# First head group's q and k built by matmuls at the start, the all-head projection moved behind the first score step, a second x buffer, and seven filler matmuls in the last batch

## The chip, the cores and the metric

The kernel runs on one core of one Trainium2 chip. The metric is device time in microseconds (us) of that core, as the median of repeated runs; lower is better. The kernels work on float32 data; matmul operands marked fp32r are float32 values read by TensorE in one pass, and precision is kept by splitting an operand into a high part (what fp32r keeps) and a low part (the rest), so that one product becomes three matmuls: high by high, high by low, low by high.

## What is computed

Eight batches of 512 tokens with 128 channels go through a macaron block: a feed-forward half step, an attention layer whose softmax is replaced by a normalised relu, and a second feed-forward half step.

```python
x = x + 0.5 * ffn(layernorm(x))                      # stage "pre" of the kernel
x = x + attention(layernorm(x))                      # 16 heads of 8 channels
x = x + 0.5 * ffn(layernorm(x))                      # stage "post"

def attention(x):
    qkv = (x @ w_qkv).reshape(B, S, 16, 24)          # q, k, v of 8 channels each
    w = relu(q @ k.T / sqrt(8))                      # 512 x 512 for each head
    out = (w / (w.sum(-1) + 1e-6)) @ v
    y = x + (out @ w_out + b_out)
    return (y - mean(y)) * rsqrt(var(y) + 1e-5) * gamma + beta

def ffn(x):                                          # 128 -> 512 -> 128, dequantised weights
    h = layernorm(x) * ln_gamma + ln_beta
    return x + 0.5 * (silu(h @ w1 + b1) @ w2 + b2)
```

## The kernel before, in words

**Attention.** The 16 heads form four groups of four. A group's q and k must lie in a form in which four heads occupy four blocks of 32 partitions (tiles `q_op` and `k_op`): each block holds the 8 channels of a head in four slots, which carry the high and low parts so that one 32-row matmul gives the sum of the products. TensorE (PE) first makes q and k of all heads at once (tasks `k` and `q`), ScalarE (ACT) copies the high part into `q_parts` and `k_parts`, VectorE (DVE) computes the low part beside it (`k_lo`, `q_lo`), and DMAs issued by SyncE (SP) spread them into `q_op` and `k_op`, four DMAs to a group.

**The loop.** A batch has 16 steps (four groups by four tiles of 128 keys). Step s issues four score matmuls (PE, line 454, into `scores`), then the value product of the step before (line 469, into `o_bank`). ACT applies the relu to two heads of a step (line 738) and DVE to the other two (line 1022). Beside these run the tasks of the neighbouring batches: the lists `PE_ORDER`, `ACT_ORDER`, `DVE_ORDER` and `POOL_ORDER` say for each step what an engine does for the batch after (`pre.*@1`) and the batch before (`post.*@-1`). Each engine runs its list strictly in the order written; semaphores order the engines. The last batch has no batch after it, so several of its steps hold only scores and values.

**The start.** Batch 0 has nothing before it to hide behind. Its `pre` stage runs by the lists `PE_FIRST`, `ACT_FIRST`, `DVE_FIRST` and `POOL_FIRST`, mostly in halves of 256 tokens (the last digit of a name). In order: `x_stats` and `x_apply` normalise, `hT` transposes, `fc1.f` multiplies (three matmuls, the third with the low part of hT), `fc2`, `xr` and `x1` form the residual, `u_apply` normalises again, `uT` transposes, then `k`, `q` and `v`. `weights.*` prepare the weights on DVE. `warm_up.n` are n matmuls of the identity with itself that have no other effect. `pre.hT@1` starts batch 1. The scores of step 0 wait until group 0's q, issued to DMA by ACT at line 703, has landed.

**The end.** `PE_LAST`, `ACT_LAST` and `DVE_LAST` finish the last batch's `post` stage in halves.

## Time and profile before

| | us |
|---|---|
| median of 3 runs | 381.1 |
| the runs | 381.10, 381.11, 379.63 |
| the profiled execution's own time | 381.01 |
| span of that execution, first to last instruction | 379.1 |
| mean granted TensorE clock | 0.991 of full |

| engine | busy us | share of the span |
|---|---|---|
| PE (matmul) | 368.6 | 97% |
| DVE | 289.8 | 76% |
| ACT | 226.6 | 60% |
| POOL | 218.5 | 58% |

Seven steady batches take 43.0 us each. The span is shorter than the device time by 1.9 us, which lie before the first and after the last recorded instruction. A busy PE in these tables counts a matmul that waits inside a group of four as busy, so 97% is not 97% of useful work. The chain that ended last runs over PE for 86% of the span; 2% are the DMA of q at the start.

### The profile page before, as it was taken

The numbers are of one execution on the slowest core, as the hardware profiler recorded it, in microseconds if no ns is written. First come the engines' busy times: TensorE is split into PE (matmuls) and PEld (weight loads), VectorE is DVE, ScalarE is ACT, GpSimd is POOL, SyncE is SP. The second block draws the span as 40 slices with busy tenths as digits, with TensorE's granted clock in tenths as the row PEclk, the third lists the DMA queues.
The fourth block names the chain that finished last, engine by engine and source line by source line (L and its number), as shares of the span: only waits on it lengthen the run. The fifth ranks groups of instructions, "written<-read, shape, count | busy, mean of one in ns | idle before, by whom it ended". The sixth has DMA issues, their size and how long they took to land.

```text
span 379.1 us, 11717 instructions
## 1 busy us (share of the span) xinstructions
PE 368.6 (97%) x4578; PEld 189.8 (50%) x4578; DVE 289.8 (76%) x698; ACT 226.6 (60%) x414; POOL 218.5 (58%) x448
## 2 busy tenths in 40 slices
PE   7979999999999999999999999999999999999997
PEld 7853524353564445553554445553454434523486
DVE  5744788897878978787878977788876976876684
ACT  3446456667846577566857476566857576465503
POOL 7674075638963589437972589438981566145041
PEclk9998999999999999999999999999999999999999
DMA  5165004500351006400361005400260005400001
GB/s 167 30 117 136 3 0 113 140 3 2 89 136 59 3 13 153 115 3 0 73 156 57 0 4 148 116 19 0 61 166 32 0 2 140 113 3 1 2 2 58
DMA packets 14390, 23.03 MB, mean 61 GB/s; under 512 B 2688, under 2 KB 3968, under 8 KB 14336
## 3 DMA queue, kind: packets, MB, share of 16 engines
q1 hardware_dynamic: 11440, 17.70, 19.1%
q10 hardware_dynamic: 2896, 4.59, 4.0%
q8 instruction: 36, 0.59, 0.7%
q14 instruction: 18, 0.15, 0.1%
HBM read 3.41 MB, written 2.10 MB: 15 GB/s over the span
## 4 chain that ended last, share of the span: by engine, by line
PE 86%; DVE 5%; DMA 3%; issue 2%; POOL 2%; ACT 1%; ACTq 0%; SPq 0%; DVEq 0%; POOLq 0%
PE o_bank L469 30%; PE scores L454 16%; PE pre_bank L412 10%; PE post_bank L412 9%; PE pre_bank L417 5%; PE pre_bank L418 3%; DMA q_op<-q_parts 2%; PE post_bank L417 2%; PE pre_bank L405 2%; PE pre_bank L431 2%; PE post_bank L431 2%; PE post_bank L418 2%; DVE probs L1022 1%; PE post_bank L405 1%; PE pre_bank L485 1%
## 5 line engine op out<-in xcount | busy, mean ns | idle before, releaser
L1022 DVE TENSOR_SCALAR probs<-scores 128x512 f32<-128x512 f32 x256 | 163.9, 682 | 50.1 <-PE scores L454 48.0
L738 ACT ACTIVATE probs<-scores 128x512 f32<-128x512 f32 x256 | 138.6, 595 | 68.9 <-PE scores L454 68.9
L469 PE MATMUL o_bank<-probs,v_op 128*32 128x512 f32 x1024 | 137.9, 611 | 0.0
L454 PE MATMUL scores<-q_op,k_op 32*128 32x512 f32 x512 | 78.4, 497 | 2.2 <-DMA q_op<-q_parts 1.7
L454 PEld LDWEIGHTS scores<-q_op,k_op 32*128 32x128 f32 x512 | 32.2, 182 | 87.2 <-issue 52.1
L628 ACT ACTIVATE pre_y<-pre_bank,b_sum,col_consts 128x512 f32<-128x512 f32 x28 | 21.8, 779 | 26.1 <-PE pre_bank L431 26.0
L469 PEld LDWEIGHTS o_bank<-probs,v_op 128*32 128x32 f32 x1024 | 21.7, 109 | 30.5 <-issue 24.5
L412 PE MATMUL pre_bank<-w,pre_y 128*32 128x128 f32 x960 | 30.8, 274 | 0.0
L412 PE MATMUL post_bank<-w,post_y 128*32 128x128 f32 x960 | 29.6, 273 | 0.0
L412 PEld LDWEIGHTS pre_bank<-w,pre_y 128*32 128x32 f32 x960 | 25.6, 110 | 7.8 <-issue 7.6
L412 PEld LDWEIGHTS post_bank<-w,post_y 128*32 128x32 f32 x960 | 26.2, 110 | 5.8 <-issue 5.7
L1051 POOL TENSOR_SCALAR norm_x_var<-norm_x_mv 128x4 f32<-128x4 f32 x21 | 4.1, 196 | 42.7 <-DVE norm_x_mv L804 42.0
L628 ACT ACTIVATE post_y<-post_bank,b_sum,col_consts 128x512 f32<-128x512 f32 x28 | 21.8, 778 | 3.5 <-PE post_bank L431 2.8
L1051 POOL TENSOR_SCALAR norm_y_var<-norm_y_mv 128x4 f32<-128x4 f32 x7 | 1.4, 199 | 37.7 <-DVE norm_y_mv L804 37.7
L1054 POOL TENSOR_TENSOR norm_x_rs<-norm_x_var,minus_half 128x4 f32<-128x4 f32 x21 | 21.2, 1010 | 1.7
L1178 POOL TENSOR_TENSOR y_rows<-y_rows,rows 128x512 f32<-128x512 f32 x7 | 9.0, 1292 | 21.0 <-ACT y_rows L662 21.0
L1132 POOL TENSOR_TENSOR v_op<-v_rows,v_op 128x128 f32<-128x128 f32 x32 | 13.7, 436 | 8.3 <-ACT v_rows L649 6.1
L1091 POOL TENSOR_TENSOR norm_x_rs<-norm_x_var,minus_half 128x4 f32<-128x4 f32 x16 | 16.4, 1024 | 1.3
L399 PE MATMUL o_bank<-ident 128*128 128x128 f32 x108 | 14.9, 300 | 1.6 <-POOL ident L1034 1.6
L399 PEld LDWEIGHTS o_bank<-ident 128*128 128x128 f32 x108 | 14.1, 213 | 2.2 <-POOL ident L1034 1.6
L1107 POOL TENSOR_SCALAR pre_xr<-pre_x,norm_x_mix 128x128 f32<-128x128 f32 x32 | 14.3, 459 | 0.8
L417 PE MATMUL pre_bank<-pre_t_hi,w_hi 128*128 128x512 f32 x28 | 14.2, 506 | 0.4 <-ACT pre_y L628 0.4
(188 smaller groups left out, 547.2 us busy)
## 6 DMA issues: line engine op xcount, KB each, us to landing
k_op<-k_parts SPq DMA_DIRECT2D x64, 128.0 KB, 2.7
q_op<-q_parts SPq DMA_DIRECT2D x62, 128.0 KB, 2.7
pre_x<-in_L_attn_x_dram ACTq DMA_DIRECT2D x7, 256.0 KB, 2.7
out_dram<-o_rows ACTq DMA_DIRECT2D x7, 256.0 KB, 2.0
w_int<-in_L_ffn_fc_q_dram SPq DMA_DIRECT2D x2, 256.0 KB, 3.9
rows<-in_lines_dram ACTq DMA_DIRECT2D x1, 256.0 KB, 5.2
s_rows<-in_L_ffn_fc_scales_dram SPq DMA_DIRECT2D x1, 256.0 KB, 6.2
q_op<-q_parts ACTq DMA_DIRECT2D x2, 128.0 KB, 3.6
```

The costliest lines, as they stand in the source:

```text
L399: mm(o_bank[1][:, 0:P], ident[:, :], ident[:, :], start=True, stop=True)
L412: last = mm(into[VW * j:VW * (j + 1), P * t:P * (t + 1)], tokens[:, part], w, start=start, stop=stop)
L417: mm(into, w_hi, t_hi, start=True, stop=False)
L418: mm(into, w_lo, t_hi, start=False, stop=False)
L431: mm(into, w1_hi[:, cols], st.t_lo[:, :], start=False, stop=True).then_inc(st.full, 1)
L454: mm(scores[i][:, j, :], k_op[rows, g, P * kt:P * (kt + 1)], q_op[rows, g, :], start=True, stop=True).then_inc(scores_done[i], 1)
L469: last = mm(o_bank[pair][VW * j:VW * (j + 1), :], v_op[:, kt, heads_of(g).start + 2 * j, :], probs[:, s % 2, j, :], start=(odd == 0 and kt ...
L628: activation(st.y[:, f, :], st.bank[:, :], ACT.Silu, bias=b1_sum[:, f:f + 1], scale=s1_col[:, f:f + 1]).then_inc(st.free, 1)
L738: activation(probs[:, s % 2, j, :], scores[0][:, j, :], ACT.Relu).then_inc(probs_done[0], 1)
L1022: v.tensor_scalar(probs[:, s % 2, 2 + j, :], scores[1][:, j, :], 0.0, None, ALU.max).then_inc(probs_done[1], 1)
L1054: p.tensor_tensor(norm.rs[:, i, :], norm.var[:, i, :], minus_half[:, i, :], ALU.pow).then_inc(norm.rs_in, 1)
L1091: p.tensor_tensor(norm.rs[:, 0, :], norm.var[:, 0, :], minus_half[:, 0, :], ALU.pow).then_inc(norm.half_in, 1)
```

## The change

Five things are changed together.

1. **Group 0 of batch 0 without copies.** POOL spreads the weights of group 0's q and k over the slots (`first_hi`, `first_lo`), so that matmuls give every slot the value directly; a per-partition factor (`sign_slot`, `low_slot`, made by DVE at the very start) turns two more passes, one by ACT and one by DVE, into the slot's high or low part, written straight into `q_op` and `k_op`. These are the parts `k0.0`, `q0.0`, `q0.1`, `k0.1`.
2. **All heads' q and k behind step 0.** `first.k.1`, `first.q.1` and `pre.hT@1` move from the start into new lists (`PE_BEGIN`, `ACT_BEGIN`, `DVE_BEGIN`) that run right after step 0 of batch 0, in full width of 512 tokens. SP copies groups 1 to 3 only. v is made in one piece of 512.
3. **A second x buffer.** Batch 1's x goes into its own buffer and is loaded by SP at the start; its statistics (`pre.x_stats@1`) move ahead of `first.xr.1` on DVE.
4. **fc1 in another order at both ends.** The high products of half 0 come first, the low products (`low.f.h`) after them, and `hT.1` stands behind half 0.
5. **Fillers.** In steps 3 to 8 and 10 of the last batch PE issues one identity matmul into the idle bank after the scores (`keep_warm`). The first warm-up stays at 12, the second goes from 9 to 7, those of 4 and 5 go, the last goes from 24 to 23.

```diff
+FIRST_PARTS = [("k0", 0), ("q0", 0), ("q0", 1), ("k0", 1)]
 PE_FIRST = [
-    "warm_up.12", "first.hT.0", "weights.b1", "first.hT.1", "first.fc1.0.0", "first.fc1.1.0", "first.fc1.0.1",
...
-    "first.fc2.3.1", "warm_up.9", "first.uT.0", "first.k.0", "first.q.0", "first.uT.1", "first.v.0", "first.k.1",
-    "first.q.1", "first.v.1", "warm_up.4", "pre.hT@1", "warm_up.5"
+    "first.fc2.3.1", "warm_up.7", "first.uT.0", "first.k0.0", "first.uT.1", "first.q0.0", "first.q0.1", "first.k0.1",
+    "first.v.1"
 ]
+PE_BEGIN = ["first.k.1", "first.q.1", "pre.hT@1"]
+BARE_STEPS = (3, 4, 5, 6, 7, 8, 10)
...
-    "pre.load_x", "weights.w1_hi", "first.hT.0", "first.hT.1", "first.fc1.0.1", "first.fc1.1.1",
-    "first.fc1.2.1", "first.fc1.3.1", "pre.load_x@1", "first.uT.0", "first.t_u.0", "first.k.0", "first.uT.1",
-    "first.q.0", "first.t_u.1", "first.k.1", "first.q.1", "first.v.0", "first.v.1", "pre.hT@1"
+    "weights.w1_hi", "first.hT.0", "first.hT.1", "first.fc1.0.1", "first.fc1.1.1",
+    "first.fc1.2.1", "first.fc1.3.1", "first.uT.0", "first.k0.0", "first.uT.1",
+    "first.t_u.0", "first.q0.0", "first.q0.1", "first.k0.1", "first.t_u.1", "first.v.1"
 ]
+ACT_BEGIN = ["first.k.1", "first.q.1", "pre.hT@1"]
...
+DVE_BEGIN = ["first.k_lo.1", "first.q_lo.1", "pre.hT@1"]
...
-    "first.x_stats.0", "first.x_stats.1", "pre.xr", "first.x1_stats.0", "first.x1_stats.1", "pre.x_stats@1",
+    "first.x_stats.0", "first.x_stats.1", "pre.xr", "weights.w_first", "first.x1_stats.0", "first.x1_stats.1", "pre.x_stats@1",
...
+            sp.dma_start(pre.x(1)[:, :, :], x_rows[1]).then_inc(x_loaded[1], 16)
...
+            def keep_warm(n):
+                pe.wait_ge(pre.free, len(PRE_FILLS) * B)
+                for _ in range(n):
+                    mm(pre.bank[:, 0:P], ident[:, :], ident[:, :], start=True, stop=True)
...
-                    pe.wait_ge(*emptied(pre, 1, "q"))
-                if kt == 0:
-                    pe.wait_ge(qk_in[g], 64 * (b + 1))
+                    pe.wait_ge(first_in, 3)
+                if b == 0 and s == TT // 2:
+                    pe.wait_ge(first_in, 4)
+                if kt == 0 and copied(g, b) > 0:
+                    pe.wait_ge(qk_in[g], copied(g, b))
...
+                    if b == 0 and s == 0:
+                        work(0, PE_BEGIN)
+                    if b == B - 1 and s in BARE_STEPS:
+                        keep_warm(1)
...
+                elif what in ("q0", "k0"):
+                    i = "qk".index(what[0])
+                    act.wait_ge(slots_ready, 2)
+                    act.wait_ge(first_made, FIRST_PARTS.index((what, h)) + 1)
+                    activation(first_high(i)[:, cols], first_bank(i, h), ACT.Copy, scale=sign_slot[:, i:i + 1]
+                               ).then_inc(first_high_in, 1)
...
+                    v.scalar_tensor_tensor((q_op, k_op)[i][:, 0, cols], first_bank(i, h), low_slot[:, i:i + 1],
+                                           first_high(i)[:, cols].bitcast(F32), ALU.mult, ALU.subtract).then_inc(first_in, 1)
...
+            def prepare_first():
+                pool.wait_ge(wqkv_ready, 1)
+                for to, of in ((first_hi, wqk_hi), (first_lo, wqk_lo)):
+                    last = p.tensor_copy(to[:, :, :].rearrange("p i (r c) -> p i r c", c=SLOTS),
+                                         of[:, :, 0:ROW].bitcast(F32).unsqueeze(3).to_broadcast([P, 2, ROW, SLOTS]))
+                last.then_inc(w_first_ready, 1)
```

How the change moves instructions shows in each engine's list. First DVE at the start, from the low part of the quantised fc1 weights (`w_lo`) to the residual; `pre_t_lo` is the low part of hT, `b_sum` the fc1 bias, `w<-w_int` the fc2 weights, `pre_xr` the residual. Before:

```order
L755 SCALAR_TENSOR_TENSOR w_lo<-w,col_consts,w_hi 128x512 [waits w_link]
L944 TENSOR_TENSOR pre_t_lo<-pre_bank,pre_t_hi 128x256 [waits pre_t_hi_first_half]
L762 TENSOR_TENSOR b_sum<-o_bank,col_consts 128x4 [waits cols_loaded,b1_added]
L764 TENSOR_TENSOR b_sum<-b_sum,col_consts 128x4 [waits b1_link]
L944 TENSOR_TENSOR pre_t_lo<-post_bank,pre_t_hi 128x256 [waits pre_t_hi_in]
L770 TENSOR_SCALAR w<-w_int 128x512 [waits w2_loaded]
...
L789 TENSOR_TENSOR wqk_lo<-wqk,wqk_hi 128x256 [waits wqk_link]
L926 SCALAR_TENSOR_TENSOR pre_xr<-rows,pre_xr 128x512 [waits rows_loaded,pre_mixed]
L949 TENSOR_TENSOR x<-pre_bank,pre_xr 128x256 [waits pre_residual,pre_full_first_half]
```

Now, on DVE in the same place:

```order
L841 SCALAR_TENSOR_TENSOR w_lo<-w,col_consts,w_hi 128x512 [waits w_link]
L1030 TENSOR_TENSOR pre_t_lo<-pre_bank,pre_t_hi 128x256 [waits pre_t_hi_first_half]
L997 TENSOR_SCALAR pre_h<-pre_x,norm_x_mv,norm_x_rs 128x128 [waits norm_x_rs_in,norm_x_measured]
...
L1030 TENSOR_TENSOR pre_t_lo<-post_bank,pre_t_hi 128x256 [waits pre_t_hi_in]
L848 TENSOR_TENSOR b_sum<-o_bank,col_consts 128x4 [waits cols_loaded,b1_added]
...
L856 TENSOR_SCALAR w<-w_int 128x512 [waits w2_loaded]
...
L875 TENSOR_TENSOR wqk_lo<-wqk,wqk_hi 128x256 [waits wqk_link]
L881 BN_STATS norm_x_stats<-pre_x 128x6 [waits x_loaded1]
...
L890 BN_AGGR norm_x_mv<-norm_x_stats 128x2 [waits norm_x_mix_in,norm_x_shift_in,norm_x_counted]
...
L1012 SCALAR_TENSOR_TENSOR pre_xr<-rows,pre_xr 128x512 [waits rows_loaded,pre_mixed]
L1035 TENSOR_TENSOR x<-pre_bank,pre_xr 128x256 [waits pre_residual,pre_full_first_half]
```

The weight preparations now stand behind the low part of hT's second half, and the statistics of batch 1's x stand ahead of the residual. Next PE, around step 0 of batch 0. Before:

```order
L412 MATMUL post_bank<-wv,t_u 32x128 [waits pre_bank_free]
...
L405 MATMUL pre_bank<-ident,pre_h 128x128 [waits pre_rows,pre_bank_free]
...
L454 MATMUL scores<-q_op,k_op 128x512 [waits qk_in0,pre_bank_free]
...
L417 MATMUL pre_bank<-pre_t_hi,w_hi 128x512 [waits pre_bank_free]
L418 MATMUL pre_bank<-pre_t_hi,w_lo 128x512
L431 MATMUL pre_bank<-pre_t_lo,w_hi 128x512
L454 MATMUL scores<-q_op,k_op 128x512 [waits probs_done0]
```

Now, on PE:

```order
L464 MATMUL pre_bank<-wv,t_u 32x128 [waits pre_bank_free,pre_free_first_half]
...
L508 MATMUL scores<-q_op,k_op 128x512 [waits first_in]
...
L469 MATMUL o_bank<-pre_t_hi,wqk_hi 128x512
L470 MATMUL o_bank<-pre_t_hi,wqk_lo 128x512
L629 MATMUL o_bank<-pre_t_lo,wqk_hi 128x512
L469 MATMUL post_bank<-pre_t_hi,wqk_hi 128x512
L470 MATMUL post_bank<-pre_t_hi,wqk_lo 128x512
L629 MATMUL post_bank<-pre_t_lo,wqk_hi 128x512
L457 MATMUL pre_bank<-ident,pre_h 128x128 [waits pre_rows,pre_bank_free]
...
L469 MATMUL pre_bank<-pre_t_hi,w_hi 128x512 [waits pre_bank_free]
```

The wait for the copies of group 0 (`qk_in0`) is gone from step 0, and six matmuls of 512 columns and the transposes of batch 1 now stand between step 0's scores and batch 1's first fc1, behind which step 1's scores come. The same place on ACT: before, the parts of q and k, the DMA and the v copies stand ahead of step 0's relus (`probs`).

```order
L695 ACTIVATE q_parts<-scores 128x256 [waits pre_bank_full]
L703 DMA q_op<-q_parts 64x1x512 [waits q_high_in,q_high_first_half]
L703 DMA q_op<-q_parts 64x1x512 [waits pre_bank_free,pre_free_first_half]
...
L624 ACTIVATE pre_t_hi<-pre_bank 128x512 [waits pre_bank_full]
L738 ACTIVATE probs<-scores 128x512 [waits scores_done0] x2
L628 ACTIVATE pre_y<-pre_bank,b_sum,col_consts 128x512 [waits pre_bank_full]
```

Now, on ACT:

```order
L779 ACTIVATE v_rows<-pre_bank 128x512 [waits pre_bank_full]
L808 ACTIVATE probs<-scores 128x512 [waits scores_done0] x2
L776 ACTIVATE k_parts<-o_bank 128x512 [waits pre_bank_full]
L776 ACTIVATE q_parts<-post_bank 128x512 [waits pre_bank_full]
L697 ACTIVATE pre_t_hi<-pre_bank 128x512 [waits pre_bank_full]
L701 ACTIVATE pre_y<-pre_bank,b_sum,col_consts 128x512 [waits pre_bank_full]
```

Three copies of 512 columns now stand between step 0's relus and batch 1's first silu.

## Rows read from the trace of the kernel before

**Rows 1.** The page: the granted TensorE clock in 40 slices.

```profile
PEclk9998999999999999999999999999999999999999
```

**Rows 2.** Chain that ended last, start: start us, length us, what.

```profile
14.74 2.20 PE o_bank L399 x18
...
20.80 0.36 ACT q_parts L695
...
21.99 4.35 DMA q_op<-q_parts
...
26.48 0.50 PE scores L454 x3
...
32.22 0.50 PE scores L454 x2
```

**Rows 3.** Stretches: length, busy PE PEld DVE ACT POOL, granted clock, DMA share, GB/s.

```profile
16.80:21.20 4.40, 3.84 (x50) 2.72 (x48) 3.18 (x15) 2.93 (x8) 3.66 (x11) 1.00 0.02 6
21.20:23.40 2.20, 1.20 (x13) 0.98 (x9) 0.41 (x2) 0.66 (x2) 0.41 (x1) 1.00 0.35 64
23.40:26.50 3.10, 1.79 (x18) 1.63 (x18) 0.69 (x1) 0.60 (x1) 2.66 (x8) 1.00 0.98 186
...
28.80:32.15 3.35, 3.35 (x12) 0.95 (x12) 0.86 (x2) 1.69 (x3) 3.35 (x4) 0.51 0.78 210
```

**Rows 4.** Timeline of DVE, start: start us, length us, [idle before <-releaser].

```profile
8.37 0.42 DVE L944 TENSOR_TENSOR pre_t_lo<-post_bank,pre_t_hi 128x256 fp32r<-128x256 f32 x1
...
12.46 0.69 DVE L926 SCALAR_TENSOR_TENSOR pre_xr<-rows,pre_xr 128x512 f32<-128x512 f32 x1 [1.22 <-POOL pre_xr L1107]
13.49 0.42 DVE L949 TENSOR_TENSOR x<-pre_bank,pre_xr 128x256 f32<-128x256 f32 x1 [0.34 <-PE pre_bank L412]
...
16.43 0.87 DVE L795 BATCH_NORM_STATS2 norm_x_stats<-pre_x 128x6 f32<-128x128 f32 x4
```

**Rows 5.** Timeline of ACT, start.

```profile
9.43 2.83 ACT L683 ACTIVATE pre_y<-scores,b_sum,col_consts 128x512 f32<-128x512 f32 x4 [1.42 <-PE scores L538]
...
26.98 1.09 ACT L738 ACTIVATE probs<-scores 128x512 f32<-128x512 f32 x2 [2.30 <-PE scores L454]
27.95 0.78 ACT L628 ACTIVATE pre_y<-pre_bank,b_sum,col_consts 128x512 f32<-128x512 f32 x1
```

**Rows 6.** Timeline of POOL, start.

```profile
7.11 0.79 POOL L1089 TENSOR_SCALAR norm_x_var<-norm_x_mv 128x4 f32<-128x4 f32 x1
...
24.00 0.20 POOL L1089 TENSOR_SCALAR norm_x_var<-norm_x_mv 128x4 f32<-128x4 f32 x1
```

**Rows 7.** Timeline of PE, start.

```profile
23.39 0.66 PE L405 MATMUL pre_bank<-ident,pre_h 128*128 128x128 f32 x4 [1.00 <-ACT v_rows L708]
...
33.54 1.07 PE L469 MATMUL o_bank<-probs,v_op 128*32 128x512 f32 x8
```

**Rows 8.** Timeline of PE, last batch, steps 8 to 10 (L454 scores, L469 values).

```profile
338.17 1.44 PE L454 MATMUL scores<-q_op,k_op 32*128 32x512 f32 x4
339.54 1.93 PE L469 MATMUL o_bank<-probs,v_op 128*32 128x512 f32 x8
341.40 0.80 PE L454 MATMUL scores<-q_op,k_op 32*128 32x512 f32 x4
342.13 1.43 PE L469 MATMUL o_bank<-probs,v_op 128*32 128x512 f32 x8
...
344.08 0.51 PE L454 MATMUL scores<-q_op,k_op 32*128 32x512 f32 x4
```

**Rows 9.** The same columns for a stretch of the last batch.

```profile
340.00:345.00 5.00, 5.00 (x36) 1.26 (x28) 1.98 (x4) 1.90 (x4) 4.64 (x12) 0.71 0.01 3
```

**Rows 10.** Timeline of DVE, last batch, steps 7 to 9.

```profile
337.80 2.61 DVE L1022 TENSOR_SCALAR probs<-scores 128x512 f32<-128x512 f32 x4
342.34 1.29 DVE L1022 TENSOR_SCALAR probs<-scores 128x512 f32<-128x512 f32 x2 [1.93 <-PE scores L454]
```

**Rows 11.** The page's DMA issues: KB each, us to landing.

```profile
w_raw<-in_L_attn_w_qkv_dram SPq DMA_DIRECT2D x1, 192.0 KB, 6.2
```

More of the change, by code:

```diff
@@ L30 @@
 ZERO_POINT = 128.0
+FIRST_FILLS = ["hT", "fc1.0", "fc1.1", "fc1.2", "fc1.3", "fc2", "uT", "v", "k", "q"]
 PRE_FILLS = ["hT", "fc1.0", "fc1.1", "fc1.2", "fc1.3", "fc2", "uT", "k", "q", "v"]
@@ L204, in build, with __init__ @@
         class Stage:
-            def __init__(self, n, fills):
+            def __init__(self, n, fills, buffers):
                 self.fills = fills
-                self.x = sb(f"{n}_x", [P, TT, D])
+                self.two_x = [sb(f"{n}_x{i}", [P, TT, D]) for i in range(buffers)]
                 self.h = sb(f"{n}_h", [P, TT, D])
@@ L536, in edge @@
                     two_products(to, w1_hi[:, weights], w1_lo[:, weights], st.t_hi[:, cols])
+                elif what.startswith("low"):
+                    f = int(what[-1])
+                    weights, to = slice(P * f, P * (f + 1)), scores[f // 2][:, f % 2, cols]
                     pe.wait_ge(*emptied(st, h, "hT"))
@@ L650, in task @@
                                    ).then_inc(pre.free, 1)
-                    elif what == "load_x" and b > 0:
-                        act.wait_ge(pre.rows, b)
-                        act.wait_ge(pre.res, b)
-                        act.dma_start(pre.x[:, :, :], x_rows[b]).then_inc(x_loaded, 16)
+                    elif what == "load_x" and b > 1:
+                        if b > 1:
+                            act.wait_ge(pre.rows, b - 1)
+                            act.wait_ge(pre.mixed, b - 1)
+                        act.dma_start(pre.x(b)[:, :, :], x_rows[b]).then_inc(x_loaded[b % 2], 16)
                     elif what in pre.fills:
@@ L738, in _ @@
                         activation(probs[:, s % 2, j, :], scores[0][:, j, :], ACT.Relu).then_inc(probs_done[0], 1)
+                    if b == 0 and s == 0:
+                        work(0, ACT_BEGIN)
                     work(b, beside)
@@ L1023, in _ @@
                                         ).then_inc(probs_done[1], 1)
+                    if b == 0 and s == 0:
+                        work(0, DVE_BEGIN)
                     work(b, beside)
@@ L1191, in work @@
                 for stage, what, tb in tasks(b, names):
-                    if (stage, what) == ("last", "mix"):
+                    if stage == "weights":
+                        prepare_first()
+                    elif (stage, what) == ("last", "mix"):
                         mix(norm_x2, tb)
```

173 lines of the change are left out of this document (107 added, 66 removed).

## The prediction

> **What bounds the kernel now.** I read the slices of the granted clock first, then the chain of waits, then timelines of the places the change touches. PE's clock is full but for one slice of 40 [rows 1], and the steady batches don't change: their PE order is the same, and PE is never waiting there for what the change moves. So only the start and the last batch can give time, and both give little: 26.5 us of the start lie before the first scores.
>
> At the start the chain runs from the high part of q (20.80) into the DMA of q, 4.35 us, and then the scores of step 0 at 26.48 [rows 2]. PE has little to do meanwhile: 1.20 of 2.20 us and 1.79 of 3.10 us busy, part of it warm-ups. Right after, from 28.80 to 32.15, its clock is 0.51, the lower of the two levels, 1.2 GHz [rows 3]. Step 2's scores come at 32.22 [rows 2]. That is the point to watch: from step 2 on the PE order is the same before and after, so the shift of step 2 is the shift of everything behind it.
>
> In the last batch a second stretch at the low level lies at about 339 to 342: the mean clock of 340 to 345 is 0.71 [rows 9], and the values of step 7 take 1.93 us [rows 8] where they take 1.07 at full clock [rows 7]. DVE then idles 1.93 us waiting for PE [rows 10]. So PE is the late one there.
>
> **The start, step by step.** Durations are those of the same operations before.
>
> *DVE, to the residual.* `hT.1` comes behind half 0 on PE. The fc1 products can begin near 7.1, since `w_lo` no longer waits behind `x_apply.1`; twelve of them at 0.12 us take 1.5, the transposes 0.4, ACT's copy 0.4, so DVE's low part of half 1 ends near 9.9, where it ended at 8.79 [rows 4]: 1.1 us later. The weight preparations stand behind it. Batch 1's statistics, about 1.2 us of DVE's time from 16.43 on [rows 4], are now ahead of the residual too. Against these 2.3 us stand the idle times of 1.22 and 0.34 us [rows 4], which are used up. What is left, with 0.2 for hand-overs, puts x1's first half at 14.4 rather than 13.49 [rows 4]: **0.95 us later**.
>
> *ACT's silus* start after the seventeenth product rather than the ninth, at 10.5 instead of 9.43, and end near 13.3 instead of 12.26 [rows 5]. fc2's last blocks move by 0.7, and DVE is the later one by then, so this adds nothing.
>
> *To step 0.* The statistics are gone from behind `u_apply.0`, but `u_apply.1` now stands ahead of uT's low part and waits for POOL. My chain: u_apply.0 16.8, uT.0 on PE 17.5, its low part 18.9, k0.0 19.4, uT.1's low part 20.6, q0.1 on PE 21.1, through ACT 21.5 and DVE 21.9, k0.1 22.25; `t_u.1` ends on ACT at 22.1. Scores would be free at 21.9, but the v product, 0.9 us, stands ahead of them on PE and waits for `t_u.1`: 22.2 to 23.1. **Step 0 at 23.1**, 3.4 us earlier than 26.48. The two copies of weights on POOL (1.5 us by the 0.79 us of its longest small operation and what 128x512 take, bounds 0.9 and 2.6) fit its idle time before x1's statistics.
>
> *To step 1.* Here most of it is given back. Before, batch 1's transposes (0.66 us, at 23.39 [rows 7]) lay under the DMA, and so did their parts. Now behind step 0's scores come k and q in full width (6 matmuls, 1.45 us) and these transposes on PE. ACT is later: v's copy ends at 23.95, two relus 1.09 [rows 5], then k, q and hT each 0.5 to 0.6, to 26.4. DVE follows with three low parts to 27.4. Batch 1's fc1.0 needs the last of them, and step 1's scores stand behind it at 27.74. Before, fc1.0 followed the scores at once and ACT's silu of it began at 27.95 [rows 5]; mine begins there too. So **the 3.4 us at step 0 are 0.1 at step 1**.
>
> *From step 1 to step 2.* Before, step 1's fc1 and values ran at the low clock. Their full durations (0.9 and 0.99 against 1.5 and 1.86, and the scores') make 1.54 us of the time to 32.22. With PE at full clock throughout, mine puts step 2 at 30.8: **1.4 us earlier**. But PE is nearly idle between the warm-ups (7 instead of 9, ending near 16.9) and v: about 1.9 us of work in 5.3, much less than the 2.99 of 5.3 that it did between 21.20 and 26.50, and the clock fell after those [rows 3]. So I expect a low stretch at the start again, only earlier. At worst it covers v, step 0 and the first of k: step 0 at 24.05, step 1 at 29.0, step 2 at 32.05, **0.1 us earlier**. At best it falls on small matmuls that wait anyway. I take 0.5 us earlier, nearer to the worst, since v and the scores are dense work right behind the idle time.
>
> *The copies* of groups 1 to 3 are issued after k's low part (26.1): four issues of 0.62 and a landing of up to 4.35 us [rows 2] make 33.1. Step 4 needs them at about 35.5. No wait.
>
> **A rule on shared ports.** While DVE computed `w_lo` from two operands in SBUF, POOL's small operation took 0.79 us at 7.11; alone it takes 0.20 at 24.00 [rows 6]. Such pairs delay each other. POOL's second weight copy may be running when DVE wants to begin the residual near 13.7, an operation with two SBUF inputs; no row shows which of the two would wait, so its price is 0 to 0.4 us at x1, inside my range. The Trainium skill (SBUF — State Buffer, "Who interferes with whom") says that whoever issues first holds the shared port pair for the whole instruction and the other fully blocks. By that rule the residual would wait for the copy, up to 0.4 us, and the sum would be 379.8 rather than 379.4.
>
> **The last batch.** A filler is one float32 matmul of 128 columns: 9 warm-ups took 2.20 us [rows 2], so 0.24 each, 1.7 for seven. Not all is paid. Where DVE has statistics or an addition besides its relus, PE waits inside a group of scores (1.44 us for 0.44 of work at 338.17 [rows 8]), and a filler before only shortens that wait. Going through steps 3 to 8, fillers add up to 0.5 us on PE by step 8, and DVE's two relu pairs from 337.80 to 340.41 [rows 10] absorb most. At full clock step 9's scores would come near 340.7 instead of 341.40, the values behind them at 341.2 to 342.2 instead of 342.13 to 343.50, and step 10 at 342.75 instead of 344.08 [rows 8]; with the filler of step 10, **1.1 us earlier**. If the fillers don't hold the clock, they cost 0.6.
>
> The reordered end (`PE_LAST`) is a wash: the first half's products start 0.4 us earlier, silu 0 can start 0.6 later, and fc2's final blocks meet both. I take 0, bounds -0.2 and +0.2. The earlier loads of later x change nothing: nobody waited for x in a steady batch.
>
> **The sum.** From the profiled execution, 381.01 (span 379.1 and 1.9 around it; the median is 381.1): 381.0 - 0.5 - 1.1 = **379.4 us**. About 0.5%, 1.9 us, is what a measurement of this kernel can tell from no change, so faster means below 379.2 and slower above 383.0.
>
> **The rivals.**
>
> *No low stretch on the path at either end.* The start gives 1.4 and the last batch 1.1: 378.5. For it: the new order does its dense work, v, step 0, k and q, in one row. Against: PE's idle start. Chance 0.22.
>
> *The fillers don't hold the clock.* Seven identity matmuls add 1.7 us of work over some 15. Then the end costs 0.6 instead of giving 1.1, and the start gives 0.5: 381.1. The warm-ups of the start are the same kind of matmul and stand for it, and the clock fell after 1.28 us of them all the same [rows 3]. Chance 0.20.
>
> *The wait only moves.* The copies of group 1 land after step 4 wants them, with a margin of 2.4 us that a landing of 6.8 us would use up. 1 us past that gives 380.4. Chance 0.05.
>
> *Slower: x of batch 1 lands late.* DVE takes batch 1's statistics ahead of the residual, so x's load, queued on SP behind the 192 KB of `w_raw`, holds up `xr.1`, x1 and everything behind them. It decides from a landing at 12.5; past 14.1 the kernel is slower than before. `w_raw` took 6.2 us to land [rows 11]. If x takes twice that from its issue near 3.1, it lands at 15.5 and the time is 382.4. Against it: 256 KB behind `w_raw` at the rate of the start is one or two us, so about 10. Together with further low stretches behind step 1 (1.5 us each), which act in the same direction, chance 0.08.
>
> **How the numbers follow.** The forecast's own case has 0.45, with 378.8 to 380.1 and two fifths of it below 379.2. Faster: 0.18 and 0.22, 0.40. Slower by over 0.5%: 0.05, a part of the last rival. Within: 0.55. For 8 in 10 the range must take in the case with no low stretch, down to 378.1 with its bounds of 0.4, and the fillers' failure up to 381.3.
>
> **What would show it.** In the changed profile: DVE's x1 at 14.4; PE's step 0 at 23 to 24 with no DMA ahead of it; step 1 near 27.7 to 29 with PE idle before fc1's low product, which waits for DVE's low part of batch 1's hT; a low stretch between 19 and 26 rather than 28.8 to 32.15; step 2 at 30.8 to 32.1. In the last batch, values of steps 7 and 8 at 1.07 us, and step 10 about 1.1 us nearer to the start of the batch's step 3. I would be wrong if the hand-overs at the start chain tighter than mine, so that step 1 follows step 0 by less than 4 us, or if the low stretch stays away.

## The result and the profile after

The changed kernel takes 386.5 us (median of 6 runs, 384.1 to 387.18), the kernel before 380.37 beside it (6 runs, 378.29 to 381.32): ratio 1.0161, 95% interval 1.0132 to 1.0190. It is 1.6% slower, outside the range of 378.1 to 381.3, on the side that had a chance of 0.05. The profiled execution took 386.52 with a span of 384.6. Two runs of the kernel before, of 384.17 and 436.22 us, were in a slower state of the chip and are left out of every figure below.

The page, as [rows 1]: the granted clock is low in two slices now.

```profile
PEclk9986999999999999999999999999999999999999
```

PE's start, as [rows 2, 7] (start us, length us, what, [idle before <-releaser]):

```profile
1.58 5.49 PE L445 MATMUL o_bank<-ident 128*128 128x128 f32 x24 [1.58 <-POOL ident L1129]
6.86 0.47 PE L581 MATMUL pre_bank<-ident,pre_h 128*128 128x128 f32 x2
...
23.72 1.62 PE L464 MATMUL pre_bank<-wv,t_u 128*32 128x128 f32 x32 [0.99 <-ACT t_u L766]
25.27 0.80 PE L508 MATMUL scores<-q_op,k_op 32*128 32x512 f32 x4
...
29.75 0.66 PE L457 MATMUL pre_bank<-ident,pre_h 128*128 128x128 f32 x4 [1.41 <-DVE q_parts L1056]
31.82 0.80 PE L469 MATMUL pre_bank<-pre_t_hi,w_hi 128*128 128x512 f32 x1 [1.41 <-DVE pre_t_lo L895]
...
33.40 0.80 PE L508 MATMUL scores<-q_op,k_op 32*128 32x512 f32 x4
...
35.91 1.94 PE L526 MATMUL o_bank<-probs,v_op 128*32 128x512 f32 x8
37.78 0.51 PE L508 MATMUL scores<-q_op,k_op 32*128 32x512 f32 x4
```

Step 0's scores stand at 25.27, 1.2 us earlier than in [rows 2], step 1's at 33.40 (27.80 before) and step 2's at 37.78, 5.6 us later than before. The whole time moves by nearly as much, 386.52 against 381.01, but only since later gains and losses cancel (below). So most of the loss is made between 25.27 and 33.40. Two things are to be seen there. PE waits 1.41 us for DVE's `q_parts` before it may transpose batch 1's h, and 1.41 us more for the low part of the same h. And seven of the ten operations of 512 columns take 0.63 to 0.80 us there, where they take 0.39 to 0.51 at full clock.

The same stretches in a view by windows (columns as [rows 3], the granted clock third from the end), with one of the last batch as [rows 9]:

```profile
18.40:23.70 5.30, 3.16 (x16) 2.17 (x17) 3.02 (x9) 2.93 (x8) 4.18 (x11) 1.00 0.01 2
23.70:27.40 3.70, 3.68 (x39) 2.63 (x40) 1.45 (x3) 1.68 (x3) 1.10 (x3) 0.55 0.02 4
27.40:31.80 4.40, 1.59 (x8) 0.83 (x6) 2.09 (x4) 1.79 (x3) 4.07 (x10) 0.89 0.27 59
31.80:37.80 6.00, 5.84 (x22) 2.18 (x22) 1.29 (x2) 2.58 (x4) 3.48 (x5) 0.50 0.82 197
...
340.00:345.00 5.00, 5.00 (x39) 1.60 (x31) 4.83 (x15) 2.78 (x6) 1.89 (x4) 1.00 0.01 3
```

PE is at the lower level, 1.2 GHz, from about 23.7 to 27.4 and again for all of 31.8 to 37.8, each time behind a stretch in which it stood partly idle. Before, there was one such stretch at the start, of 3.35 us [rows 3].

DVE at the same place:

```profile
15.48 0.42 DVE L1035 TENSOR_TENSOR x<-pre_bank,pre_xr 128x256 f32<-128x256 f32 x1
...
28.31 0.69 DVE L1056 SCALAR_TENSOR_TENSOR k_parts<-o_bank,k_parts 128x512 fp32r<-128x512 f32 x1 [0.90 <-ACT k_parts L776]
29.00 0.69 DVE L1056 SCALAR_TENSOR_TENSOR q_parts<-post_bank,q_parts 128x512 fp32r<-128x512 f32 x1
31.07 0.69 DVE L895 TENSOR_TENSOR pre_t_lo<-pre_bank,pre_t_hi 128x512 fp32r<-128x512 f32 x1 [1.38 <-ACT pre_t_hi L697]
```

The low parts of k and q end at 29.69; the transposes, which write another bank (`pre_bank`), start at 29.75, since `next_fill` waits until all ten fills of batch 0 have been read. From there one engine waits for the other again: ACT copies the transposed h, DVE makes its low part at 31.07, and only then, at 31.82, can PE begin fc1.

A second loss stands behind step 2, at full clock. From step 2 of batch 0 to step 2 of the last batch the changed kernel takes 294.24 us and the kernel before 293.58. Of this, 1.2 us are lost in the first steps of batch 1 and 0.6 are given back later. In batch 1 PE waits for the copy of q and then for `aT`, the transposed attention output:

```profile
70.44 0.50 PE L508 MATMUL scores<-q_op,k_op 32*128 32x512 f32 x4 [0.43 <-DMA q_op<-q_parts]
...
76.82 1.08 PE L464 MATMUL post_bank<-wo,aT 128*32 128x128 f32 x32 [0.72 <-DVE aT L920]
```

`aT` is late since DVE's product ahead of it, `a_t`, takes 1.24 us. In the same trace, at 67.47, it takes 0.41. POOL had begun an addition 0.33 us before it. POOL, then DVE:

```profile
74.36 1.28 POOL L1220 TENSOR_TENSOR pre_xr<-pre_xr,b_quarter 128x512 f32<-128x512 f32 x1
```

```profile
74.69 1.24 DVE L914 TENSOR_TENSOR a_t<-o_t,rec 128x256 f32<-128x256 f32 x1
75.96 0.71 DVE L920 STREAM_TRANSPOSE aT<-a_t 128x512 f32<-128x512 f32 x1
```

Both operations read two operands from SBUF. In `idle_filled`, an experiment below, DVE begins 0.19 us before POOL, and PE waits at neither place:

```profile
70.31 0.42 DVE L918 TENSOR_TENSOR a_t<-o_t,rec 128x256 f32<-128x256 f32 x1
```

```profile
70.50 1.37 POOL L1224 TENSOR_TENSOR pre_xr<-pre_xr,b_quarter 128x512 f32<-128x512 f32 x1
```

The pair of waits, with `a_t` at 0.96 to 1.48 us, is in the profiled executions of the changed kernel, `ht_wait_v`, `xstats_back`, `fc1_order_back`, `three_back` and `k_in_gap`, and there the stretch from step 2 to batch 1's step 4 is 1.3 us longer than in `idle_filled` (1.6 in `xstats_back`). In the profiles of the kernel before, of `no_fillers` and of the six others it is absent. How many of the unprofiled runs have it, and why q's copy lands later in those six, stays open.

In the last batch PE's scores of step 2 and of step 10 in the changed kernel, with the fillers:

```profile
332.02 0.51 PE L508 MATMUL scores<-q_op,k_op 32*128 32x512 f32 x4
...
349.37 0.50 PE L508 MATMUL scores<-q_op,k_op 32*128 32x512 f32 x4
```

And step 2 in the kernel before, whose step 10 is in [rows 8]:

```profile
325.73 0.50 PE L454 MATMUL scores<-q_op,k_op 32*128 32x512 f32 x4
```

The same two steps in `no_fillers`, the changed kernel without the fillers:

```profile
329.59 0.51 PE L508 MATMUL scores<-q_op,k_op 32*128 32x512 f32 x4
...
346.41 0.50 PE L508 MATMUL scores<-q_op,k_op 32*128 32x512 f32 x4
```

The DMA issues of the page after, the load of batch 1's x (KB, us to landing):

```profile
pre_x<-in_L_attn_x_dram SPq DMA_DIRECT2D x1, 256.0 KB, 7.3
```

### The profile page after: what moved, and what is told of

Same layout as the page of the kernel before. It is cut to its first block, busy times and chain, and to the rows that moved or that the text cites. A ratio compares the mean times of both kernels' runs of the same rounds, so it can differ in the third digit from the quotient of the medians.

```text
span 384.6 us, 11723 instructions
## 1 busy us (share of the span) xinstructions
PE 370.2 (96%) x4574; PEld 191.3 (50%) x4574; DVE 293.4 (76%) x705; ACT 227.8 (59%) x415; POOL 218.1 (57%) x450
## 4 chain that ended last, share of the span: by engine, by line
PE 88%; DVE 6%; ACT 2%; issue 1%; DMA 1%; POOL 1%; SPq 0%; POOLq 0%; DVEq 0%; ACTq 0%
PE o_bank L526 30%; PE scores L508 16%; PE pre_bank L464 9%; PE post_bank L464 9%; PE pre_bank L469 5%; PE o_bank L445 3%; PE pre_bank L470 2%; PE post_bank L469 2%; PE pre_bank L457 2%; DVE probs L1115 2%; PE post_bank L470 2%; PE post_bank L483 2%; PE pre_bank L483 2%; PE post_bank L457 1%; PE pre_bank L542 1%
## 5 line engine op out<-in xcount | busy, mean ns | idle before, releaser
L508 PE MATMUL scores<-q_op,k_op 32*128 32x512 f32 x512 | 76.0, 499 | 0.7 <-DMA q_op<-q_parts 0.4
L508 PEld LDWEIGHTS scores<-q_op,k_op 32*128 32x128 f32 x512 | 31.0, 183 | 83.8 <-issue 50.2
L469 PE MATMUL pre_bank<-pre_t_hi,w_hi 128*128 128x512 f32 x28 | 14.6, 520 | 2.0 <-DVE pre_t_lo L895 1.4
L445 PE MATMUL o_bank<-ident 128*128 128x128 f32 x84 | 12.7, 321 | 1.6 <-POOL ident L1129 1.6
L914 DVE TENSOR_TENSOR a_t<-o_t,rec 128x256 f32<-128x256 f32 x16 | 13.2, 825 | 0.0
```

The source lines that it names most:

```text
L445: mm(o_bank[1][:, 0:P], ident[:, :], ident[:, :], start=True, stop=True)
L469: mm(into, w_hi, t_hi, start=True, stop=False)
L508: mm(scores[i][:, j, :], k_op[rows, g, P * kt:P * (kt + 1)], q_op[rows, g, :], start=True, stop=True).then_inc(scores_done[i], 1)
```

## The experiments

Two theories stood against each other. **Queues:** the start's orders (batch 1's hT waiting for all fills, its statistics ahead of the residual, `hT.1` behind half 0) push step 1 out. **Clock:** PE's idle places let its clock fall under the dense work behind them. A third theory was that the fillers of the last batch cost more than they give. All ratios are against the kernel before, run beside each, with a 95% interval; the last column is the granted clock over the run, from run to run.

| kernel | median us | ratio | steps 0, 1, 2 at | clock of the runs |
|---|---|---|---|---|
| before | 380.37 | 1 | 26.48, 27.80, 32.15 | 0.985 to 1.00 |
| changed | 386.5 | 1.0161 (1.0132 to 1.0190) | 25.27, 33.40, 37.78 | 0.982 to 0.991 |
| fillers_only | 379.52 | 1.0016 (0.9979 to 1.0054) | 26.48, 27.82, 30.68 | 0.990 to 1.00 |
| no_fillers | 385.82 | 1.0166 (1.0091 to 1.0241) | 25.04, 32.12, 36.31 | 0.982 to 0.991 |
| ht_wait_v | 382.63 | 1.0075 (1.0037 to 1.0113) | 24.83, 30.98, 33.81 | 0.987 to 1.00 |
| xstats_back | 384.55 | 1.0130 (1.0053 to 1.0206) | 24.20, 31.42, 35.80 | 0.991 |
| fc1_order_back | 386.36 | 1.0131 (1.0070 to 1.0191) | 23.70, 31.69, 36.02 | 0.982 to 0.987 |
| three_back | 382.64 | 1.0061 (1.0027 to 1.0095) | 25.14, 31.37, 34.20 | 0.991 to 1.00 |
| idle_filled | 381.44 | 1.0032 (0.9998 to 1.0066) | 24.54, 31.07, 33.89 | 1.00 |
| k_in_gap | 381.87 | 1.0052 (1.0023 to 1.0081) | 23.45, 28.51, 32.84 | 0.991 to 0.996 |
| three_filled | 378.76 | 0.9978 (0.9949 to 1.0007) | 23.86, 28.92, 31.74 | 1.00 |
| k_gap_filled | 378.92 | 0.9965 (0.9936 to 0.9995) | 23.51, 28.57, 31.40 | 1.00 |
| before_start_filled | 379.62 | 0.9985 (0.9957 to 1.0014) | 26.64, 27.97, 30.85 | 0.990 to 1.00 |
| before_filled | 378.36 | 0.9977 (0.9947 to 1.0006) | 27.13, 28.46, 31.32 | 0.995 to 1.00 |

### The fillers of the last batch

`fillers_only` is the kernel before with nothing but them, `no_fillers` the changed kernel without them.

```diff
                     step_scores(b, s)
+                    if b == B - 1 and s in (3, 4, 5, 6, 7, 8, 10):
+                        keep_warm(1)
                     work(b, early)
```

> The kernel before with the seven filler matmuls of the last batch alone. Theory A (the fillers keep the clock full in the last batch, and the loss lies wholly in the start): about 1.0 us faster than before, values of step 7 at 1.07 us instead of 1.93, no low stretch near 340. Theory B (the last batch's clock changed by chance, the fillers only cost time): 0 to 0.6 us slower than before.

> The changed kernel without the seven fillers. Theory A: 1.0 us slower than the changed kernel, so about 7 us slower than before, with a low stretch in the last batch. Theory B: no change against the changed kernel or up to 0.6 us faster.

Neither pair differs by what a measurement can tell: 1.0016 against 1, and 1.0166 against 1.0161. The loss isn't theirs. The low stretch that `no_fillers` was expected to show in the last batch is not in its profile: the granted clock from 325 to 350 is 1.00. So its trace gives the fillers' price. From the last batch's step 2 to its step 10 it takes 16.82 us; with the fillers it is 17.35 in the changed kernel and 17.33 in `fillers_only`. In the two profiles with a low stretch there, `before` and `before_start_filled`, it is 18.35 and 18.33. So the fillers save 1.0 us in an execution that would have had the low stretch, and cost 0.5 us in one that would not.

### Batch 1's transposes wait for v alone

```diff
                 if what == "hT":
-                    next_fill(st, b, "hT")
+                    if st is pre and b == 1:
+                        pe.wait_ge(*emptied(pre, 1, "v"))
+                    else:
+                        next_fill(st, b, "hT")
```

> The changed kernel, but PE's transposes of batch 1 (hT@1) wait only until v has left the bank they write, and no longer for DVE's low parts of k and q. Theory A (this queue is a part of the loss): the idle time of 1.41 us ahead of them goes, ACT's copy and DVE's low part follow 0.7 to 1.4 us earlier, and the kernel is 1 to 1.5 us faster than the changed one; up to 3 if the second low stretch goes as well. Theory C (the clock alone decides): PE's idle time only moves behind the transposes and the time stays within 0.5 us.

PE's start in `ht_wait_v`:

```profile
27.92 0.60 PE L457 MATMUL pre_bank<-ident,pre_h 128*128 128x128 f32 x4
30.09 0.50 PE L469 MATMUL pre_bank<-pre_t_hi,w_hi 128*128 128x512 f32 x1 [1.57 <-DVE pre_t_lo L898]
...
30.98 0.50 PE L511 MATMUL scores<-q_op,k_op 32*128 32x512 f32 x4
...
33.81 0.51 PE L511 MATMUL scores<-q_op,k_op 32*128 32x512 f32 x4
```

The transposes stand 1.8 us earlier, with no wait. Step 2 stands 4.0 us earlier, and fc1's products take 0.50 again: in this execution the second low stretch is gone too. The ten runs have clocks from 0.987 to 1.00, so not all need be like it. The kernel gains 0.86% (1.0161 to 1.0075), 3.3 us, near the "up to 3" that was expected with the second stretch gone. The wait is one cause; this run can't say how much of the gain is the wait and how much the clock.

### The two other orders

`xstats_back` puts batch 1's statistics behind `u_apply.0` again, `fc1_order_back` puts `hT.1` and `x_apply.1` back where they were (DVE's list is shown; PE's has `first.hT.1` ahead of fc1 again, whose blocks alternate between the halves):

```diff
-    "weights.w_qkv", "pre.x_stats@1", "first.xr.1", ... "first.u_apply.0", "first.u_apply.1",
+    "weights.w_qkv", "first.xr.1", ... "first.u_apply.0", "pre.x_stats@1", "first.u_apply.1",
```

```diff
-    ... "first.x_apply.0", "weights.w1_lo", "first.hT.0", "first.x_apply.1", "first.hT.1", "weights.b1",
+    ... "first.x_apply.0", "first.x_apply.1", "weights.w1_lo", "first.hT.0", "weights.b1", "first.hT.1",
```

> The changed kernel, but batch 1's statistics go back to their old place on DVE, behind u_apply.0; the second buffer and its early load stay. Theory A (DVE is the late engine from the residual on): x1 on DVE 1.1 us earlier (near 14.3 instead of 15.48), step 0 by 0.5 to 1.1 us earlier, since the statistics then fit DVE's wait for POOL. Theory C (PE, not DVE, is the late one there): x1 waits for fc2 and moves by less than 0.5 us, the total by less than 0.3.

> The changed kernel with the start's fc1 products and DVE's tasks around them in the order of before (low products right behind their high ones, hT.1 ahead of them, x_apply.1 ahead of w_lo); everything else as changed. Theory A (DVE waits for hT.1's high part and its weight tasks queue behind): fc2's first block near 11.1 instead of 12.32, x1 on DVE about 1 us earlier than 15.48, the kernel 0.8 to 1.3 us faster than the changed one. Theory C (the start's clock alone): within 0.3.

x1 moves by 1.1 and 1.9 us and step 0 by 1.1 and 1.6, but not all of it is the orders' doing. The first twelve warm-ups were shorter in these two executions, and `hT.0` came at 6.42 and 6.11, not 6.86. Against `no_fillers`, where it came at 6.46 and x1 at 14.93, the statistics' old place gives 0.6 us (14.36); `fc1_order_back` has no such partner. Neither edit moves the kernel by more than its interval, where 0.8 to 1.3 us had been expected of the second. In both traces the transposes still wait for `q_parts` (1.47 and 1.41 us) and a second low stretch follows. `fc1_order_back` shows also what the two engines behind one port do. DVE in `fc1_order_back`:

```profile
12.63 0.85 DVE L1012 SCALAR_TENSOR_TENSOR pre_xr<-rows,pre_xr 128x512 f32<-128x512 f32 x1
13.59 0.42 DVE L1035 TENSOR_TENSOR x<-pre_bank,pre_xr 128x256 f32<-128x256 f32 x1
```

POOL in it:

```profile
12.55 0.39 POOL L1145 CAST first_hi<-wqk_hi 128x256 fp32r<-128x256 f32 x1
12.89 0.85 POOL L1145 CAST first_lo<-wqk_lo 128x256 fp32r<-128x256 f32 x1
```

The first copy takes its 0.39 us, the residual begun under it 0.85 where it takes 0.69 in [rows 4] and 0.66 in the changed kernel, and the second copy, issued under the residual, 0.85. It takes 0.40 in the changed kernel. The x1 of this kernel is only 0.1 later than before.

### All three back

> The changed kernel with the three edits together: hT@1 waits for v only, the statistics back, the fc1 order back. Group 0 is still made by PE and k, q of all heads still stand behind step 0. Theory A (three DVE queues are the loss, and they add up): x1 near 13.5 as before, step 0 near 22.5, step 2 near 31, the kernel within 1 us of before, on either side. Theory D (the detour through PE, ACT and DVE for group 0 and the work behind step 0 cost by themselves): still 2 us or more slower than before.

1.0061: hardly better than `ht_wait_v` alone (1.0075), although x1 stands at 14.03, not 15.23. That is 2.3 us slower than the kernel before, where theory A expected at most 1, and step 0 stands at 25.14, not near 22.5. Its runs differ by their clock: six at 0.991 with a median of 383.38, one at 1.00 with 379.82. In its profile v takes 1.94 us and the clock from 23.7 to 27.4 is 0.50. With the queues mended, the clock is what is left to test, beside the 1.3 us of batch 1, which this profile has too.

### The idle places filled

`idle_filled` is the changed kernel with more identity matmuls in PE's waits of the start; every wait stays. `warm_bank` puts them into `pre_bank` once v is copied:

```diff
-    "first.fc2.3.1", "warm_up.7", "first.uT.0", "first.k0.0", "first.uT.1", "first.q0.0", "first.q0.1", "first.k0.1",
-    "first.v.1"
+    "first.fc2.3.1", "warm_up.8", "first.uT.0", "warm_up.2", "first.k0.0", "first.uT.1", "first.q0.0", "warm_up.2", "first.q0.1", "first.k0.1",
+    "warm_up.4", "first.v.1"
-PE_BEGIN = ["first.k.1", "first.q.1", "pre.hT@1"]
+PE_BEGIN = ["first.k.1", "first.q.1", "warm_bank.6", "pre.hT@1", "warm_up.6"]
```

> The changed kernel with identity matmuls put where PE is idle at the start: 2 behind uT.0, 2 behind q0.0, 4 ahead of v, 6 behind q of all heads, 6 behind batch 1's transposes, and 8 instead of 7 warm-ups. No wait is shortened. Theory C (the low clock is a large part of the loss): both low stretches go, v takes 0.9 instead of 1.6 us, step 1's products run at full clock, and the kernel is 2.5 to 4 us faster than the changed one. Theory A (the queues are the loss, the clock only a little): 0 to 1 us faster, or slower by what the fillers add.

PE's start in `idle_filled`:

```profile
23.53 1.08 PE L464 MATMUL pre_bank<-wv,t_u 128*32 128x128 f32 x32
24.54 0.51 PE L508 MATMUL scores<-q_op,k_op 32*128 32x512 f32 x4
...
28.11 0.66 PE L457 MATMUL pre_bank<-ident,pre_h 128*128 128x128 f32 x4
...
31.07 0.51 PE L508 MATMUL scores<-q_op,k_op 32*128 32x512 f32 x4
...
33.89 0.51 PE L508 MATMUL scores<-q_op,k_op 32*128 32x512 f32 x4
```

All ten runs are at clock 1.00, and the ratio falls from 1.0161 to 1.0032, by 4.9 us, more than the 2.5 to 4 expected. Step 2 stands 3.9 us earlier, though nothing but useless matmuls was added. So the clock is the other cause. Of the 5.4 us between the two profiled executions 1.3 are the waits of batch 1, which this one doesn't have; whether the fillers keep them away or chance does isn't shown. By the ratios the fillers alone give more than the three orders alone (1.0032 against 1.0061), but the two intervals overlap.

### k of all heads ahead of v

`k_in_gap` is `three_back` with `first.k.1` moved from behind step 0 into PE's wait ahead of v.

```diff
-    "first.v.1"
+    "first.k.1", "first.v.1"
-PE_BEGIN = ["first.k.1", "first.q.1", "pre.hT@1"]
+PE_BEGIN = ["first.q.1", "pre.hT@1"]
```

> The kernel of three_back, with k of all heads (three matmuls of 512 columns) made ahead of v, in PE's idle time of about 1 us before t_u.1. Theory A: 0.5 to 0.7 us faster than three_back, since PE's work behind step 0 shrinks and k's parts are ready earlier. Theory E (behind step 0 the last to arrive is DVE's low part of batch 1's hT, behind ACT's copies and DVE's relus, not PE): no change against three_back, within 0.3.

PE's start in `k_in_gap`:

```profile
23.45 0.51 PE L513 MATMUL scores<-q_op,k_op 32*128 32x512 f32 x4
...
27.62 0.50 PE L471 MATMUL pre_bank<-pre_t_hi,w_hi 128*128 128x512 f32 x1 [2.33 <-DVE pre_t_lo L903]
...
28.51 0.51 PE L513 MATMUL scores<-q_op,k_op 32*128 32x512 f32 x4
...
30.98 1.93 PE L531 MATMUL o_bank<-probs,v_op 128*32 128x512 f32 x8
32.84 0.54 PE L513 MATMUL scores<-q_op,k_op 32*128 32x512 f32 x4
```

Here the start is nearly as the prediction drew it, step 0 at 23.45 (23.1 forecast) and step 1 at 28.51 (27.74), with clock 1.00 up to there. But PE now waits 2.33 us in one piece for DVE, and the low stretch follows behind it, on step 1's values (1.93 us). 1.0052 is within the interval of `three_back`, so the run doesn't decide between the two theories.

### Both causes taken away

> The three edits of three_back (batch 1's hT waits for v alone, its statistics back behind u_apply.0, the old order of hT.1 and fc1) together with identity matmuls in PE's idle places of the start (warm_up.8, 2, 2 and 4 around the first products, 6 behind batch 1's transposes). If clock and queues are two separate costs, their gains add: all runs at clock 1.00, step 2 near 33.3, and 379.8 us, the time of the one run of three_back that was at full clock (379.82). If what the three edits gave was only that one low stretch went away with them, the fillers leave them nothing: 381.4 us as in idle_filled.

> k_in_gap (k of all heads ahead of v) with such matmuls: warm_up.8, 2 and 1 around the first products and nine behind batch 1's transposes, in PE's wait of 2.33 us. Without a low stretch its step 2 should come at 31.0 (28.51 for step 1 and 2.4 to 2.5 for a step at full clock), against 30.68 of the kernel before at full clock: 378.8 us, nothing left of the 3.4 us that step 0 is earlier. If step 0's lead were worth something once the clock holds, it would be 377 or less. If the nine matmuls hold up the first fc1 product, 379.5.

`three_filled` is `three_back` with the fillers of `idle_filled`, but none ahead of batch 1's transposes; those behind them go into a free bank. `k_gap_filled` is the like of `k_in_gap`:

```diff
-    "first.fc2.3.1", "warm_up.7", "first.uT.0", "first.k0.0", "first.uT.1", "first.q0.0", "first.q0.1", "first.k0.1",
+    "first.fc2.3.1", "warm_up.8", "first.uT.0", "warm_up.2", "first.k0.0", "first.uT.1", "first.q0.0", "warm_up.1", "first.q0.1", "first.k0.1",
-PE_BEGIN = ["first.q.1", "pre.hT@1"]
+PE_BEGIN = ["first.q.1", "pre.hT@1", "warm_o.9"]
```

378.76 and 378.92 us, all 24 runs at clock 1.00. Against the changed kernel that is 1.8 and 2.0%, 7 us and more. `three_filled` is a microsecond under the 379.8 expected, and its step 2 stands at 31.74, not near 33.3. By the ratios the fillers alone took away 1.29%, the three orders alone 1.00%, both together 1.83%. That is less than the sum, as it should be if part of what the wait's removal gave was a low stretch that went with it, but the gap of 0.46% is within the noise of four ratios. So the shares depend on the order of counting: fillers first, they give 4.9 us and the orders 2.0; orders first, they give 3.8 us and the fillers 3.2.

`k_gap_filled` stands 0.35% under the kernel before, and its interval just leaves out 1. By what the medians show, that is the steadier clock and not the new start: the runs of the kernel before that are at full clock have a median of 378.46 us (below), which is no more than 378.92. PE in `k_gap_filled`, at step 1:

```profile
25.19 2.17 PE L669 MATMUL o_bank<-ident 128*128 128x128 f32 x18
27.68 0.50 PE L471 MATMUL pre_bank<-pre_t_hi,w_hi 128*128 128x512 f32 x1 [0.31 <-DVE pre_t_lo L907]
...
28.57 0.51 PE L513 MATMUL scores<-q_op,k_op 32*128 32x512 f32 x4
```

Nine fillers lie in the wait of 2.33 us, and 0.31 is left of it.

### The same for the kernel before

```diff
-    "first.fc2.3.1", "warm_up.9", "first.uT.0", "first.k.0", ...
+    "first.fc2.3.1", "warm_up.9", "first.uT.0", "warm_up.2", "first.k.0", ...
-    "first.q.1", "first.v.1", "warm_up.4", "pre.hT@1", "warm_up.5"
+    "first.q.1", "first.v.1", "warm_up.7", "pre.hT@1", "warm_up.9"
```

> The kernel before with identity matmuls in the waits of its start only: 2 more behind uT.0, 7 instead of 4 ahead of batch 1's transposes, 9 instead of 5 behind them. If the low stretch of 28.80 to 32.15 comes from the idle places ahead of it, it is gone in every run, and what is left of low clock is the last batch's: 378.9 us, runs between 378.3 and 379.6, ratio 0.997. If the low stretches are due to something else (the phase of the run), the clocks of the runs spread as those of the kernel before: ratio 1.000.

> The same and the seven fillers of the last batch. All runs at clock 1.00: 378.4 us, ratio 0.995, faster than both kernels. If the fillers of the last batch cost as much as they give, as fillers_only had it on average, 379.0. If the start's matmuls stand in the way of the scores of step 0, whose DMA lands at 26.3: 379.5 or more.

With matmuls in the start's waits the low stretch of [rows 3] is absent from both profiles; since that of `fillers_only` lacks it as well, with no matmul added at the start, this alone doesn't show that they took it away. Windows of `before_start_filled`, start and last batch:

```profile
26.50:32.00 5.50, 5.36 (x29) 2.57 (x29) 3.09 (x5) 4.07 (x8) 5.35 (x9) 1.00 0.86 202
335.00:340.00 5.00, 4.90 (x25) 1.37 (x25) 3.55 (x12) 1.64 (x4) 3.37 (x9) 0.77 0.00 0
```

The one of the last batch stays, and 5 of 12 runs are under 0.999, down to 0.990. The median of 379.62 is above the 378.9 expected, so that expectation failed. With the seven fillers too (`before_filled`) it is 1 of 12, and 378.36 us is the lowest median of all. Its interval takes in 1, so that it beats the kernel before can't be said; nor can `before_filled`, `three_filled` and `k_gap_filled` be told apart.

How much the clock matters is seen in the kernel before itself. Its runs from these studies, sorted by their granted clock: 39 at 0.999 or 1.00 have a median of 378.46 us, 22 at 0.995 or 0.996 one of 380.1, 12 at 0.99 one of 381.1, and 4 at 0.985 to 0.987 one of 382.9. So one step down in these groups is 1 to 2 us.

## Why the prediction was wrong

Of the 7.1 us between 379.4 and the profiled 386.52, 6.1 lie ahead of step 2, which the forecast put at 31.65 and which came at 37.78, and 1.0 behind it.

**The step "To step 1" failed: a wait was missing.** It let batch 1's transposes follow q's products on PE, at about 25.1, with ACT to 26.4 and DVE to 27.4 behind them. They wait for DVE's low parts of k and q, which the same step had listed as DVE's work. In the lists ahead of the prediction the transposes did show `waits pre_rows,pre_bank_free`; the prediction did not ask how far `pre_bank_free` has to count. From step 0 to step 1 it said 4.64 us; measured 8.13. With both causes gone it is 5.06 (`three_filled`), with the clock held and the wait left 6.53 (`idle_filled`). So of the 3.5 us too much, some 1.5 are the wait, 1.6 the clock, and 0.4 the estimate.

**"A low stretch at the start again, only earlier" failed in number.** The place was right: `v`, step 0 and the first of k at 0.55. So was the reason, as far as the runs show it: PE idled ahead of v, though it was busy 3.16 of 5.30 us there, where the forecast had 1.9. The prediction saw that PE would idle again ahead of fc1's low product, but took nothing from it for the clock. The 1.41 and 1.41 us that PE was idle there were followed by a second stretch, 31.8 to 37.8, on fc1, step 1 and its values. The slower rival had "further low stretches behind step 1 (1.5 us each)" only beside a late x. Its condition never came to pass; x landed in 7.3 us from its issue at 3.2, 3 us ahead of its need at 13.52. The stretches came without it. They should have been a rival of their own.

**DVE's 0.95 us was too small.** x1 stands at 15.48, forecast 14.44. In the profiled run of the changed kernel the twelve warm-ups took 5.49 us, 4.57 in that of the kernel before, and `hT.0` came at 6.86 instead of 5.98. The kernel before takes this lightly: with `hT.0` at 6.77 its x1 is at 13.70 (`before_start_filled`). The changed order passes it on. At like warm-ups the new order so costs 1.8 us, and `no_fillers`, with `hT.0` at 6.46, has x1 at 14.93. From x1 to v it is 8.24 rather than 7.8; the four copies on ACT whose scale is a column took 0.47 to 0.49 us each, those with none 0.38 to 0.39.

**The start's gain of 0.5 rested on one picture of the kernel before.** Its low stretch of [rows 3] is there in the profiled run, and absent in the profile of `fillers_only`, whose start is the same code: step 2 at 30.68. Half of the runs of before are at 0.999 or 1.00. What the change could win by moving it, the kernel before has in every second run.

**"The shift of step 2 is the shift of everything behind it" failed.** The PE order is the same from there on, but DVE and POOL meet in another order in batch 1, and 1.2 us are lost there (see the result).

**The last batch was right in the trace, and half luck.** From its step 2 to its step 10 the scores stand 17.35 us apart (332.02 to 349.37), 18.35 before (325.73 to [rows 8]'s 344.08): 1.0 us, forecast 1.1, and the clock is 1.00. But the 1.1 is again the price of a stretch that not every run has: `no_fillers` has clock 1.00 there without fillers and is through 0.5 us sooner. So the 0.6 us that the rival gave as the fillers' cost was a good estimate, for an execution that has no low stretch there. The medians agree: at 0.999 or 1.00 the seven runs of `fillers_only` have 378.91 us, the kernel before 378.46. Between saving 1.0 and costing 0.5 the fillers gave nothing that `fillers_only` can show.

**"3.4 us at step 0 are 0.1 at step 1"** was the right thought. At full clock and with the wait gone, step 0 stands 3.1 and 2.8 us earlier than before, step 1 0.6 and 0.95 later, step 2 0.55 and 0.9 later (`k_gap_filled` and `three_filled` against `before_start_filled`): what is won by dropping the copies through DMA is spent again on work that used to lie under them and now stands behind step 0.

**The shared port.** In the changed kernel the weight copies (13.66 and 14.00, 0.40 us each) ended before the residual began at 14.71, so the case named didn't arise. It did in `fc1_order_back`, above: 0.2 us on the residual, 0.46 on POOL's second copy. The prediction looked for such pairs only here. The dear one was the pair of batch 1, where DVE's `a_t` took 0.83 us longer. The Trainium skill (SBUF — State Buffer, "Who interferes with whom") has the later one wait for the holder; it says so of a DVE instruction in a two-port mode, and of one with two SBUF inputs, as these are, that it contends. The rows agree on who waits, but not on a wait for the holder's whole length: the residual ends 0.54 us after the first copy (alone it takes 0.66), the second copy 0.26 after the residual (alone 0.40), `a_t` 0.29 after POOL's addition (alone 0.41).

## What to carry to other kernels

When work is moved behind a new first step, read each moved instruction's wait down to the count that it waits for: a wait for "all fills" ties a transpose to copies of other banks. Before a change is costed from one profile, sort the runs of the kernel by granted clock; a gain or loss that only undoes a low stretch is worth its share of the runs. And where PE waits for others at a start, count the idle time as a risk for the dense work behind it, and cover it with matmuls into a bank that is free: here that gave 4.9 us by itself. Where the clock would have held anyway, such matmuls cost time, 0.5 us for the seven of the last batch. And don't take it that a shift at the start is carried through unchanged: look at the places behind it where two engines begin operations within a few tenths of a microsecond of each other.
